# Keys and queries of six batches as three rounded products instead of one full product

## The reference, cut to what matters

```python
x: (8, 512, 128) float32                        # 8 batches of 512 tokens, width 128
n = layernorm(x)
q, k, v = split(n @ W_qkv + b_qkv)              # 16 heads of 8; window of 32 tokens
attn = softmax(q @ k.T / sqrt(8), masked) @ v
x = x + attn @ W_out + b_out
x = x + moe(layernorm(x))                       # shared expert plus top-1 of 7 experts
```

## Time and profile before

| | |
|---|---|
| median of 3 runs | 327.05 us (326.39 to 329.93) |
| the profiled execution's own time | 329.34 us |
| its span, first to last instruction | 327.6 us |
| PE busy | 298.1 us (91%) |
| DVE busy | 224.7 us (69%) |
| POOL busy | 175.0 us (53%) |
| ACT busy | 147.3 us (45%) |
| mean granted TensorE clock | 0.968 |

### The profile page before, as it was taken

How to read it: one execution, slowest core, us unless ns; L and a number is a source line. 1 busy time by engine, 2 the same in 40 slices (tenths; PEclk the granted TensorE clock), 3 DMA queues, 4 the chain that set the end, 5 groups by cost and what they waited for, 6 DMA issues and landing times. The chain is left out here.

```text
span 327.6 us, 11893 instructions
## 1 busy us (share of the span) xinstructions
PE 298.1 (91%) x4834; PEld 244.8 (75%) x4834; DVE 224.7 (69%) x438; ACT 147.3 (45%) x230; POOL 175.0 (53%) x277
## 2 busy tenths in 40 slices
PE   8899999999799897999983489999989999999994
PEld 8646676576566474678872378888989999999994
DVE  6699999898588797777961153466558778775442
ACT  3434556444344673782720012253345555556530
POOL 7797585723127652910277604444438666764344
PEclk9999999999799999999995589999999999999999
DMA  7961422414041422099412201114244544343320
GB/s 194 349 157 48 111 57 85 105 52 108 20 118 47 109 51 62 5 395 335 133 52 104 102 0 68 66 66 75 58 80 85 99 82 89 67 97 79 76 52 26
DMA packets 52504, 32.47 MB, mean 99 GB/s; under 512 B 25424, under 2 KB 46676, under 8 KB 52450
## 3 DMA queue, kind: packets, MB, share of 16 engines
q1 hardware_dynamic: 47968, 23.18, 28.7%
q0 software_dynamic: 2880, 6.43, 5.6%
q10 hardware_dynamic: 1602, 2.10, 2.0%
HBM read 13.72 MB, written 11.95 MB: 78 GB/s over the span
## 5 line engine op out<-in xcount | busy, mean ns | idle before, releaser
L682 POOL DMA_INDIRECT out<-y,xn_base x38 | 39.6, 1041 | 37.7 <-DVE y L1366 35.4
L777 ACT ACTIVATE Pr<-psS 128x1024 f32<-128x1024 f32 x32 | 32.8, 1025 | 31.3 <-PE psS L1472 31.3
L1114 DVE TENSOR_TENSOR hT<-psS,PT 128x512 f32<-128x512 f32 x32 | 22.3, 696 | 34.9 <-remote 11.9
L859 ACT ACTIVATE PT<-psS 128x512 f32<-128x512 f32 x32 | 19.0, 597 | 55.3 <-PE psS L1606 47.9
L1351 DVE TENSOR_TENSOR Pr<-psS,PT 128x512 f32<-128x512 f32 x38 | 26.0, 685 | 23.4 <-PE psS L1745 9.9
L963 DVE TENSOR_REDUCE row_max<-psS 128x16 fp32r<-128x1024 f32 x32 | 37.7, 1218 | 4.8 <-PE psS L1460 4.7
L892 ACT ACTIVATE PT<-psS 128x512 f32<-128x512 f32 x38 | 22.7, 597 | 39.5 <-PE psS L1735 16.9
L1733 PE MATMUL psS<-xT_hi,taken_parts 128*128 128x256 f32 x128 | 38.5, 301 | 0.0
L1018 DVE STREAM_TRANSPOSE PT<-Pr 128x1024 f32<-128x1024 f32 x32 | 37.3, 1205 | 0.0
L649 POOL DMA_INDIRECT sorted_rows<-rows,pos_u x24 | 23.0, 959 | 25.4 <-DVE rows L1119 19.0
L1734 PE MATMUL psS<-xT_lo,taken_parts 128*128 128x256 f32 x128 | 36.1, 282 | 0.0
(11 more groups left out here) (223 smaller groups left out, 681.3 us busy)
## 6 DMA issues: line engine op xcount, KB each, us to landing
sorted_rows<-pad_rows SPq DMA_DIRECT2D x9, 528.0 KB, 5.3
xn_base<-sorted_rows SPq DMA_DIRECT2D x38, 66.0 KB
rows<-in_L_attn_x SPq DMA_DIRECT2D x8, 256.0 KB, 6.5
xs<-sorted_rows SPq DMA_DIRECT2D x64, 32.0 KB
VD_even<-V SPq DMA_DIRECT2D x28, 72.0 KB
VD_odd<-V SPq DMA_DIRECT2D x28, 72.0 KB
w_sb<-in_L_ffn_w_gate ACTq DMA_DIRECT2D x1, 1792.0 KB, 11.8
Kx<-K SPq DMA_DIRECT2D x28, 64.0 KB
```

Of the source, the lines that this page charges most:

```text
L682: pool.indirect_dma_start(out=out_list, out_offset=bass.IndirectOffsetOnAxis(tok_u[:, r, :], 0), in_=y[:, r, :], in_offset=None, bounds_ch ...
L777: nc.scalar.activation(Pr[:, half, :], psS[:, half, :], ACT.Exp, scale=SCALE).then_inc(exp_done, 1)
```

## The change

The program keeps a rounded copy of the turned tokens (`xnT_hi`, written by ScalarE from the same bank right behind `xnT`) and the rest (`xnT_lo`, a subtraction on GpSimd, `low_columns`). The key and query weights are split likewise, once, on GpSimd (`split_wqk`). From batch 2 on each of keys and queries is three rounded products into the same bank instead of one full product. Batches 0 and 1 and all values stay as they were.

```diff
--- before.py
+++ after.py
@@ -65,6 +65,7 @@
     PADS = 4
     RING = 4
     PLACES = 4
+    ROUNDED = 2
     NOBODY = 2 * NT * P
     EARLY_TILES, LATE_TILES = slice(0, NT - LATE * TPB), slice(NT - LATE * TPB, NT)
     ALPHA, EPS = 2.0, 1e-5
@@ -133,6 +134,10 @@
         xn = xn_base[:, 0 : TPB * D].rearrange("p (k d) -> p k d", d=D)
         base = xn_base[:, :].rearrange("p (r d) -> p r d", d=ROW)
         xnT = sb("xnT", [P, T])
+        xnT_hi = sb("xnT_hi", [P, T], f32r)
+        xnT_lo = sb("xnT_lo", [P, T], f32r)
+        wqk_hi = sb("wqk_hi", [P, 2, D], f32r)
+        wqk_lo = sb("wqk_lo", [P, 2, D], f32r)
         hT = sb("hT", [P, NC, T])
         Qx = sb_over("hT", "Qx", [P, 2, T])
         Kx = sb("Kx", [P, 2, HPG, BLK + T])
@@ -237,6 +242,7 @@
         first_k_ready, first_v_ready = sem("first_k_ready"), sem("first_v_ready")
 
         norm_done, xt_done, xnT_ready = sem("norm_done"), sem("xt_done"), sem("xnT_ready")
+        xnT_hi_ready, xnT_lo_ready, wqk_split = sem("xnT_hi_ready"), sem("xnT_lo_ready"), sem("wqk_split")
         q_done, k_done, v_done = sem("q_done"), sem("k_done"), sem("v_done")
         q_ready, k_ready, v_ready = sem("q_ready"), sem("k_ready"), sem("v_ready")
         v_in = [sem(f"v_in{h}") for h in range(2)]
@@ -527,6 +533,23 @@
                 xb = x_all[:, n * TPB : (n + 1) * TPB, :]
                 pool.tensor_tensor(xb, xb, attn_bias[:, :, :].to_broadcast([P, TPB, D]), ALU.add).then_inc(xb_done, 1)
 
+            def low_columns(n):
+
+                pool.wait_ge(xnT_hi_ready, n - ROUNDED + 1)
+                pool.wait_ge(q_done, n)
+                pool.wait_ge(k_done, n)
+                pool.tensor_tensor(
+                    xnT_lo[:, :], xnT[:, :], xnT_hi[:, :].bitcast(f32), ALU.subtract
+                ).then_inc(xnT_lo_ready, 1)
+
+            def split_wqk():
+                pool.wait_ge(wqk_ready, 2)
+                pool.tensor_copy(wqk_hi[:, :, :], wqk_sb[:, :, :]).then_inc(wqk_split, 1)
+                pool.wait_ge(wqk_split, 1)
+                pool.tensor_tensor(
+                    wqk_lo[:, :, :], wqk_sb[:, :, :], wqk_hi[:, :, :].bitcast(f32), ALU.subtract
+                ).then_inc(wqk_split, 1)
+
             def residual(p):
                 pool.wait_ge(proj_ready, p + 1)
                 pool.wait_ge(xb_done, p // PPB + 1)
@@ -586,7 +609,11 @@
             EARLY, SPLITS = 5 * PPB, PPB
             for p in range(EARLY):
                 b, h = divmod(p, PPB)
+                if p == 0:
+                    split_wqk()
                 residual(p)
+                if h == 0:
+                    low_columns(b + 2)
                 if h == 0 and b + 3 < B:
                     normalise(b + 3)
                 if p == 0:
@@ -617,6 +644,7 @@
             moments(0, G1, st2_done, G1)
             deviations(0, G1 // 2)
             residual(EARLY)
+            low_columns(EARLY // PPB + 2)
             deviations(G1 // 2, G1)
             shifts(0, G1, norm2_ready)
             add_bias(B - 1)
@@ -738,6 +766,8 @@
                     act.wait_ge(v_done, n)
                     act.wait_ge(k_done, n)
                 nc.scalar.copy(xnT[:, :], psA[:, :]).then_inc(xnT_ready, 1)
+                if n >= ROUNDED:
+                    nc.scalar.copy(xnT_hi[:, :], psA[:, :]).then_inc(xnT_hi_ready, 1)
 
             def evict_q(n, odd, first=False):
                 act.wait_ge(q_done, n + 1)
@@ -1405,8 +1435,20 @@
                     last = nc.tensor.transpose(psA[:, k * P : (k + 1) * P], xn[:, k, :], ident[:, :])
                 last.then_inc(xt_done, 1)
 
+            def rounded_columns(bank, which, n):
+
+                if n == ROUNDED:
+                    pe.wait_ge(wqk_split, 2)
+                pe.wait_ge(xnT_lo_ready, n - ROUNDED + 1)
+                mm(bank, wqk_lo[:, which, :], xnT_hi[:, :], start=True, stop=False)
+                mm(bank, wqk_hi[:, which, :], xnT_lo[:, :], start=False, stop=False)
+                return mm(bank, wqk_hi[:, which, :], xnT_hi[:, :], start=False, stop=True)
+
             def queries(n):
                 pe.wait_ge(xnT_ready, n + 1)
+                if n >= ROUNDED:
+                    rounded_columns(psA[:, :], 0, n).then_inc(q_done, 1)
+                    return
                 mm(psA[:, :], wqk_sb[:, 0, :], xnT[:, :], start=True, stop=True).then_inc(q_done, 1)
 
             def keys(n):
@@ -1418,6 +1460,9 @@
                 if n >= 2:
                     pe.wait_ge(v_ready, n - 1)
                     pe.wait_ge(proj_ready, n * PPB - 3)
+                if n >= ROUNDED:
+                    rounded_columns(psB[:, :], 1, n).then_inc(k_done, 1)
+                    return
                 mm(psB[:, :], wqk_sb[:, 1, :], xnT[:, :], start=True, stop=True).then_inc(k_done, 1)
 
             def values(n):
```

## The result

| | before | after |
|---|---|---|
| median, same chip, same hour | 326.72 us (325.75 to 329.93, 4 runs) | 333.55 us (332.67 to 333.95, 4 runs) |
| profiled execution, span | 329.34, 327.6 us | 333.67, 331.9 us |

A forecast was written before the change was run, and what follows sets the result against it. The attention loop was taken as a ring of VectorE's row maxima and TensorE's scores, with keys and queries on the path in even pairs. +1.5 - 1.3 + 0.0 = +0.2 gave 327.2 us, range 324.2 to 330.6.

The forecast's parts named there:

- The wait in pair 2: Pair 2: TensorE's keys wait for GpSimd's subtraction, 1.97 us later; net cost +1.5 us.
- The clock: Rival: pair 2's new idle time makes TensorE's clock fall, +1.6 us, total 328.8; chance 0.15 alone.
- The products: Keys and queries: three rounded products take 0.70 us against 0.86, saving 0.32 a batch; pair 6 gains 0.0.
- late low halves: Rival: the low half is late in every even pair, pairs 4 to 12 lose their gain, total 328.5; chance 0.12.
- four passes: Rival: a full product passes the array four times, so 0.11 us more a batch, total 326.7; within the forecast's 0.45.
- ScalarE's cast and the weights' split: Attention loop: the rounded copy on ScalarE and the weights' split on GpSimd hide behind other work, costing nothing.
- Behind the loop nothing is touched, so a shift of the loop goes through unchanged: After the attention loop: later stages gain or lose nothing, so the loop's +0.2 us is the whole change.
- Idle times put to issue move: Rival: 24 more TensorE instructions move stalls, total 323.6 to 330.8; chance 0.13 fewer, 0.15 more (or clock and lateness together).

The follow-up runs named there:

- b_warm: The changed kernel with 24 small matmuls filling TensorE's wait in pair 2, the wait itself kept; 309.26 us, ratio 0.9992 to the kernel before.
- g_shift: The changed kernel with 12 more warming matmuls ahead of the loop; 331.97 us, ratio 1.009 to the kernel before.
- f_shift: The kernel before with 12 more warming matmuls ahead of the loop; 330.23 us, ratio 1.0066 to the kernel before.
- e_wait_full: The kernel before's full products, with keys and queries of batches 2 to 7 waiting for the low half as in the change; 313.62 us, ratio 1.0079.
- after_3: The changed kernel repeated, not altered, on another chip; 313.79 us, ratio 1.0078 to the kernel before.
- b_warm_4: The changed kernel with 24 small matmuls in TensorE's wait of pair 2, repeated on another chip; 329.93 us, ratio 0.9999 to the kernel before.
- after_2: The changed kernel repeated, not altered, on another chip; 312.48 us, ratio 1.0066 to the kernel before.
- before_2: The kernel before, unaltered, timed against itself; 309.11 us, ratio 0.9957.
- d_side: The changed kernel with full products back, all added ScalarE and GpSimd work kept, only queries waiting for the rounded copy; 310.63 us, ratio 1.0036 to the kernel before.
- i_up_late: The kernel before with seven 256 KB loads of the experts' up weights moved behind the attention loop; 327.51 us, ratio 0.9984.
- a_from3: The changed kernel with keys and queries rounded from batch 3 on, batch 2 a full product; 310.45 us, ratio 0.997 to the kernel before.

## Why the prediction was wrong, step by step

**The wait in pair 2** (+1.5): right. With the clock kept the pair costs 8.85 - 7.5 = 1.35 in b_warm and 8.89 - 7.43 = 1.46 between g_shift and f_shift. TensorE's row says 1.75 us of idling where the working had 1.97, but it counts from the end of the matmul before. From start to start the keys came 2.13 us behind that matmul, against 0.22 in before: 1.91 later, close to the 1.97. The working also let VectorE's statistics end at 38.42 where its own rows have the next row maxima start at 38.33, a slip of 0.1 us without weight in the sum.

**The clock** (named as a rival, +1.6, chance 0.15, not in the sum): this is the first step that failed. It fell in the change's profiled execution on three of four chips, and in e_wait_full, for 1.6 us. The step weighed it by idle times of 2.13 (fell) and 1.28 (kept) and took "against it that TensorE was full up to that point". The length of an idle time does not decide in this range. Over the 20 traces there are 14 idle times in the loop from 1.50 to 2.28 us: the clock fell behind seven (1.55, 1.74, 1.75, 1.75, 1.75, 1.81, 2.13) and was kept behind seven (1.50, 1.54, 1.67, 1.71, 1.75, 1.87, 2.28). Behind a single one of 1.0 to 1.47 in the loop it never fell. It did fall once ahead of the loop, in after_3, about 1.6 us behind one of 1.10, and twice in the loop's last pair, in g_shift and b_warm_4, behind one of 0.95 and one of 0.60 close together. All 20 traces have these two, and the other 18 kept the clock. By these counts, an estimate made afterwards, the sum should have carried half of 1.6. The page "TensorE: Matmul & The Clock Gate" of the Trainium skill (Part 1) says that what watches the array runs freely and does not start with the kernel; by that rule equal idle times can end differently, and the traces agree, with 1.75 us on either list.

**The products** (-0.32 a batch): right in size. 0.69 us for three, 0.23 each at full clock. Pairs 4, 6, 8, 10 and 12 on chip B, after_2 against before_2: -0.39, -0.48, -0.22, -0.25, -0.98, the last with 0.7 less idle time put to issue. Pair 6 gained too where 0.0 was forecast: its low half was ready at 65.52 on the first chip, the keys came at 66.52. The rival of late low halves is out: in pairs 4 to 12 the keys start 0.21 to 0.33 us behind the matmul before them in the four traces of the change, and 0.22 in before, so they wait 0.11 us at most. So is that of four passes, as the three cost 0.69.

**ScalarE's cast and the weights' split** (nothing): right. The second exponential of pair 2 began at 34.42 (not moved by the forecast 0.4; the pair ran 0.2 us earlier), and d_side, with all this side work, has pair 2 at 7.53.

**"Behind the loop nothing is touched, so a shift of the loop goes through unchanged"**: this is the second step that failed. 36 more instructions (12 weight loads, 12 matmuls and 12 waits; the prediction counted 24) bring every later fetch of TensorE's program forward. One of them now falls on the scatter that the experts wait for, which costs about 1.3 us and is in all four traces of the change. On the first chip it was 1.8 of the 3.8 us that were lost there; the 1.85 in the down projection is the other half, and comes from how long the clock stood at half.

**Idle times put to issue move** (rival): true, with no net sign in the loop that these runs can tell. Those of 0.3 us and more add up to 4.8 us in before and 4.9 in after, 2.7 in before_2 and 2.9 in after_2, and the one kernel before has 4.6 on chip D. Such an idle time is an instruction fetch that comes too late: in each loop there are 24 fetches of 16 KB, one every 3.3 to 7.9 us, and all 115 idle times of this kind in the 20 loops end 2.2 to 3.1 us behind the start of one. The DMA view of 81 to 84.5 us has the one ahead of the idle 2.13 of before, and then the one ahead of the 1.55 of d_side:

```profile
q8 instruction: 1, 0.02, 3.1%
```

```profile
q8 instruction: 1, 0.02, 1.7%
```

that is 3.1% and 1.7% of 16 engines for 3.5 us, 1.7 and 0.95 us for the same 16 KB. What makes one late was not found; i_up_late shows that it is not the 256 KB loads alone. The page "Runtime: NRT & Kernel Launch" of the Trainium skill (Instruction fetch mechanics) has the cost of such a refill mostly hidden. The traces agree with "mostly": 115 of 480 fetches left an idle time of 0.3 us or more, the longest 2.28.

The sum with the steps mended, where before takes about 310 us: +1.4 wait, +0.8 to 1.6 clock, -1.6 products, +1.3 `xs`, that is 1.9 to 2.7 us. Measured were 2.1 (chip B) and 2.8 (chip D) against the runs of before. The first chip's 4.9 by the ratio lies above it by 2.2 or more, of which the down projection's 1.85 is one part; chip E's four runs do not tell. The term for `xs` was found in these same traces, so this sum explains and does not test.

a_from3, the rounded products without pair 2's wait, is better than the change itself by 1.1% and 1.05% (308.99 to 312.48, 310.50 to 313.79). That it beats before is not shown: 0.997, 0.9919 and 0.998 on three chips, only chip B's interval leaves out 1, and there before itself came out at 0.9957.

## What to carry to other kernels

Where a change gives the bound engine a new wait, price the wait and what the clock may do behind it, and fill the wait with idle matmuls or take the work out of that place. Before reading a difference of under 1% as the work's own, run the old kernel against itself: here that gave 0.4% once. Instructions that are added as a control are harmless only off the path: the 12 of f_shift cost 0.67 us by themselves. And follow a lengthened program past the changed part, to the DMAs on which later stages wait.

## What the runs showed of the hardware

- Behind idle times of 1.5 to 2.3 us TensorE's clock fell in seven of fourteen cases, and their length does not tell which.
- All 115 idle times of 0.3 us and more in the loop that are put to issue end 2.2 to 3.1 us behind the start of a 16 KB fetch of instructions.
- A 16 KB instruction fetch between an indirect scatter and its landing went with 4.3 instead of 2.4 us to land (after_2, before_2), and so in five of the eleven traces with a fetch between the scatter and the loads' landing (4.3 to 4.5 us from the scatter to SyncE's load). In those five the scatter's last one or three packets started only as the fetch ended.
- Chips differ by 5%. Most of it is one stretch: from pair 15 to the experts' first block it is 79.8 us on chip B and 96.6 on the first, for the kernel before, 16.8 of the 21.8 us between the two spans. There VectorE shows, four times in 20 us, idle times that no chip of the 310 us kind has:

```profile
175.40 0.69 DVE L1114 TENSOR_TENSOR hT<-psS,PT 128x512 f32<-128x512 f32 x1 [6.24 <-remote]
180.26 0.69 DVE L1114 TENSOR_TENSOR hT<-psS,PT 128x512 f32<-128x512 f32 x1 [3.58 <-PE psS L1606]
186.60 0.69 DVE L1114 TENSOR_TENSOR hT<-psS,PT 128x512 f32<-128x512 f32 x1 [5.65 <-remote]
```

What "remote" was is open; the stall was there in before and after alike.
